# Four gathers at a time on GpSimd, each group held for two more query evictions of VectorE at a layer's head

## The chip, the core and the metric

The kernel runs on one core of a Trainium2 chip. The metric is device time in microseconds of one execution. A separate profiled execution, in which the hardware profiler records every instruction, gives the rows below.

## What is computed

A graph network on 3125 nodes and 100000 edges that are sorted by destination: four attention layers (8 heads of 16) and then one message layer. The part that the change touches is the attention over edges:

```python
def _transformer_conv(h, src, dst, Wq, bq, Wk, bk, Wv, bv, Ws, bs, Wbeta):
    q = (h @ Wq.T + bq)[dst].reshape(-1, HEADS, D_HEAD)
    k = (h @ Wk.T + bk)[src].reshape(-1, HEADS, D_HEAD)
    v = (h @ Wv.T + bv)[src].reshape(-1, HEADS, D_HEAD)
    alpha = jnp.sum(q * k, axis=-1) / float(np.sqrt(D_HEAD))
    amax = jax.ops.segment_max(alpha, dst, num_segments=n)
    ex = jnp.exp(alpha - amax[dst])
    denom = jax.ops.segment_sum(ex, dst, num_segments=n)
    a = ex / (denom[dst] + 1e-16)
    out = jax.ops.segment_sum((a[:, :, None] * v).reshape(-1, f), dst, num_segments=n)
    x_r = h @ Ws.T + bs
    beta = jax.nn.sigmoid(jnp.concatenate([out, x_r, out - x_r], axis=-1) @ Wbeta.T)
    return beta * x_r + (1.0 - beta) * out

for i in range(L):                      # L = 4
    res = h
    h = _transformer_conv(...)
    h = _layer_norm(h + res, ln_g[i], ln_b[i])
    h = gelu(h @ W1[i].T + b1[i]) @ W2[i].T + b2[i] + h
```

The message layer behind it gathers once more by source, adds what belongs to the destination, applies silu and takes the mean by destination.

## The kernel before

The nodes lie in NB = 25 blocks of 128. The edges are cut into 806 places of at most 128 edges, each place with edges of one block of destinations only. Sixteen places are a chunk (CHUNKS = 51; the last has six places), and a chunk has NG = 4 groups of G = 4 places.

All engines are programmed by hand, each with its own stream, and meet in semaphores. One attention layer runs so:

- **Head.** TensorE multiplies the 25 blocks with the key and value weights; VectorE evicts them (L1458) and SyncE stores them to `kv_table` in HBM in five pieces (L392, semaphore `tab_out`). Then come the queries: TensorE's `queries` (L966, two matmul passes a block, and a transpose, L970) alternates over two banks, and VectorE evicts each block in `begin_layer` (L1464) into `qs`, counting `q_ev`. TensorE's next block waits until `q_ev` says that the last-but-one is out of its bank. Behind the 25th eviction VectorE clears `acc` (L1467), makes the first one-hot tiles (L1249), takes 25 gate products (L1476), and multiplies chunk 0's keys with the queries (L1282) in four groups.
- **Gathers.** GpSimd (POOL) fetches each place's 128 rows of keys and values from `kv_table` with one indirect DMA (L508, in `gather_chunk`). The destination `slots` is a ring of RING = 4 chunks, so 64 gathers can run ahead. A gather waits for `tab_out` (the layer's table is stored), for `idx_in` (its indices are there), and per group for `slot_free`, which TensorE's last use of those four places releases (L825).
- **Chunks.** In `attend_step` of chunk n VectorE weighs chunk n's values (L1361), adds 16 partial sums to `acc` (L1265), and in between multiplies and sums chunk n+1's keys (L1282, L1288; each L1282 waits for `kv_in`, that is, four gathers landed, and for the spread queries of TensorE, L806). TensorE's add-ups are L825, ScalarE makes one-hot tiles.
- **Behind the last chunk** come gate, norm and feed-forward in five groups of five blocks, and the next layer's head.

Layer 0 is special: its gathers start as soon as the indices are in place, while VectorE still prepares the edge lists (L1607 to L1645); the first query eviction follows behind those. The message layer uses the same `gather_chunk` with `src_table`.

Of the kernel before, what the change touches and what calls it, by code (L numbers as in the profile page):

```python
# [25 lines left out]
L = 4  # L26
HEADS, DH = 8, 16
HID = HEADS * DH
NB = -(-N // P)
# [10 lines left out]
NG = CH // G  # L40
# [16 lines left out]
START = (RING - 1) * NG + 1  # L57
# [19 lines left out]
def build_program(nc, a, out):  # L77
    with ExitStack() as ctx:
# [3 lines left out]
        def sem(name):  # L82
            return ctx.enter_context(nc.semaphore(name))
# [166 lines left out]
        in_ps, in_act, s_ps, q_ev, h_ev = sem("in_ps"), sem("in_act"), sem("s_ps"), sem("q_ev"), sem("h_ev")  # L250
# [57 lines left out]
        def turn_of(l, i, k, j=0):  # L308

            return l * (FULL + (k < REM - 1 or (k == REM - 1 and j < LAST_NG))) + i  # L310
# [166 lines left out]
        @block.gpsimd  # L477
        def _(pool):


            for s in counted:
                pool.sem_inc(s, START)
            pool.wait_ge(su_idx, 1)
            for c in range(VC):
                pool.indirect_dma_start(row_sets[:, c, :], None, a["edge_t"],
                                        bass.IndirectOffsetOnAxis(ap=vti[:, c:c + 1], axis=0)).then_inc(su_rows, 16)
            uses = [[pool.alloc_register(f"uses{k}_{j}") for j in range(NG)] for k in range(RING)]
            for k in range(RING):
                for j in range(NG):
                    pool.reg_mov(uses[k][j], 0)  # L490

            def gather_chunk(k, turn, l, table, width, places=CH):
                groups = -(-places // G)
                used = [pool.snap(uses[k][j]) for j in range(groups)]
                if k == 2:
                    pool.wait_ge(su_termsd, 48)
                if k == 3:
                    pool.wait_ge(su_rstd, 16 * 2 * HEADS)
                pool.wait_ge(tab_out, 16 * NI * (l + 1))
                pool.wait_ge(idx_in[k], 16 * (turn + 1))  # L500
                for j in range(groups):
                    if isinstance(turn, int):
                        pool.wait_ge(slot_free[k][j], START + turn)
                    else:
                        pool.wait_ge(slot_free[k][j], START + used[j])
                        pool.reg_add(uses[k][j], uses[k][j], 1)
                    for t in range(j * G, min((j + 1) * G, places)):
                        pool.indirect_dma_start(slots[:, k, t, 0:width], None, table,  # L508
                                                bass.IndirectOffsetOnAxis(ap=idx[:, k, t:t + 1], axis=0))\
                            .then_inc(kv_in[k][j], 16)  # L510

            def gather_rest(l, table, width):
                for k in range(REM):
                    gather_chunk(k, turn_of(l, FULL, k), l, table, width, min(CH, PLACES - (RING * FULL + k) * CH))

            with pool.Fori(0, L) as l:
                with pool.Fori(0, FULL) as i:
                    for k in range(RING):
                        gather_chunk(k, turn_of(l, i, k), l, kv_table, KVW)
                gather_rest(l, kv_table, KVW)  # L520
            with pool.Fori(0, FULL) as i:
                for k in range(RING):
                    gather_chunk(k, turn_of(L, i, k), L, src_table, HID)
            gather_rest(L, src_table, HID)

            def root(sums, out, nth):

                pool.wait_ge(var_ans, START + 2 * nth)
                pool.tensor_tensor(guarded[:, :], sums, eps[:, :], ALU.add).then_inc(var_ans, 1)
                pool.wait_ge(var_ans, START + 2 * nth + 1)  # L530
                pool.tensor_tensor(out, guarded[:, :], half_power[:, :], ALU.pow).then_inc(var_ans, 1)

            pool.wait_ge(acc_done, START + CH * (L * CHUNKS + CHUNKS - 3))
            for i in range(NI):
                pool.memset(hidden[i][64:XW, :], 1.0).then_inc(hid_one, 1)
            for nth, (i, m) in enumerate(ASKED):
                pool.wait_ge(var_ready, START + nth + 1)
                root(var_of[2 * i + m], inv_of[2 * i + m], nth)
# [1271 lines left out]
```

## Time and profile before

| | us |
|---|---|
| time, median of 3 runs | 5614.84 (5613.83 to 5617.6) |
| profiled execution: span from the first to the last instruction | 7840.1 |
| PE / VectorE / ScalarE / POOL busy in it | 4625.7 / 4037.4 / 2769.9 / 3849.3 |
| mean granted TensorE clock in it | 0.679 |

For the profiled execution no time but its span is given. It is 40% longer than the runs without a profile. In the rows, "<-X" behind an idle time names what ended it; "remote" and "another core or an unknown queue" mean that the semaphore was raised by nothing that the profile can name, "issue" that the engine waited for nothing that it shows.

### The profile page before, as it was taken

The numbers are of one execution on the slowest core, as the hardware profiler recorded it, in microseconds if no ns is written. First come the engines' busy times: TensorE is split into PE (matmuls) and PEld (weight loads), VectorE is DVE, ScalarE is ACT, GpSimd is POOL, SyncE is SP. The second block draws the span as 40 slices with busy tenths as digits, with TensorE's granted clock in tenths as the row PEclk, the third lists the DMA queues.
The fourth block names the chain that finished last, engine by engine and source line by source line (L and its number), as shares of the span: only waits on it lengthen the run. The fifth ranks groups of instructions, "written<-read, shape, count | busy, mean of one in ns | idle before, by whom it ended". The sixth has DMA issues, their size and how long they took to land.

```text
span 7840.1 us, 106032 instructions
## 1 busy us (share of the span) xinstructions
PE 4625.7 (59%) x22831; PEld 3727.9 (48%) x22832; DVE 4037.4 (51%) x11107; ACT 2769.9 (35%) x6493; POOL 3849.3 (49%) x4066
## 2 busy tenths in 40 slices
PE   4555555655556556555555565555555656666667
PEld 2444444534444445344444453444444545555555
DVE  4555555645555556455555565555555553333334
ACT  1333333423333334233333342333333432323333
POOL 3555555335555553345555543455555425555553
PEclk6666666676666666766666667666666677877887
DMA  5222222222322222222223222222322211111111
GB/s 127 78 79 76 77 76 78 52 66 73 79 78 77 78 80 56 69 67 79 76 78 79 78 62 69 68 78 77 80 78 79 60 33 43 44 44 44 44 44 30
DMA packets 267188, 536.13 MB, mean 68 GB/s; under 512 B 116253, under 2 KB 148689, under 8 KB 266509
## 3 DMA queue, kind: packets, MB, share of 16 engines
q0 software_dynamic: 180992, 490.24, 23.6%
q1 hardware_dynamic: 78901, 35.89, 1.9%
q10 hardware_dynamic: 6936, 6.69, 0.3%
q14 instruction: 314, 2.57, 0.1%
q8 instruction: 45, 0.74, 0.0%
HBM read 512.41 MB, written 18.03 MB: 68 GB/s over the span
## 4 chain that ended last, share of the span: by engine, by line
PE 26%; another core or an unknown queue 26%; issue 20%; DVE 17%; ACT 5%; DVEq 4%; ACTq 1%; SPq 0%; DMA 0%; POOL 0%; POOLq 0%
PE bank L806 9%; PE bank L825 7%; DVE acc L1265 6%; ACT oh L556 2%; DVEq L333 2%; PE bank L797 2%; PE bank L851 2%; PE bank L810 1%; DVE alpha L1288 1%; PE bank L879 1%; DVEq L1265 1%; DVE slots L1361 1%; DVE oh L1249 1%; PE bank L1001 1%
## 5 line engine op out<-in xcount | busy, mean ns | idle before, releaser
L508 POOL DMA_INDIRECT slots<-kv_table,idx x3224 | 3065.2, 951 | 3133.0 <-PE bank L825 1275.8
L825 PE MATMUL bank<-slots,oh 128*128 128x136 f32 (+1 forms) x8060 | 1593.0, 351 | 569.1 <-DVE acc L1265 506.4
L806 PE MATMUL bank<-qs,ohT 128*128 x8080 | 1685.7, 356 | 235.1 <-ACT ohT L547 129.2
L825 PEld LDWEIGHTS bank<-slots,oh 128*128 128x128 f32 x8060 | 1411.7, 252 | 704.7 <-DVE acc L1265 608.2
L806 PEld LDWEIGHTS bank<-qs,ohT 128*128 128x128 f32 x8080 | 1434.4, 257 | 456.6 <-issue 434.4
L1265 DVE TENSOR_TENSOR acc<-acc,bank 128x136 f32 (+1 forms) x4030 | 1172.0, 291 | 614.6 <-PE bank L825 171.5
L1282 DVE TENSOR_TENSOR slots<-slots,bank 128x512 f32<-128x512 f32 x808 | 551.8, 683 | 1322.6 <-remote 1291.5
L547 ACT ACTIVATE ohT<-bank,miss 128x512 f32<-128x512 f32 x1010 | 676.7, 683 | 1367.9 <-PE bank L797 1234.5
L508 POOL DMA_INDIRECT slots<-src_table,idx x806 | 760.4, 943 | 756.9 <-DMA idx<-src_e 247.9
L843 PE MATMUL bank<-ident,alpha 128*128 128x128 f32 x204 | 93.7, 459 | 1487.2 <-DVE alpha L1288 1481.7
L556 ACT ACTIVATE oh<-iota,rel_e 128x128 f32<-128x128 f32 x3168 | 962.8, 387 | 0.0
L843 PEld LDWEIGHTS bank<-ident,alpha 128*128 128x128 f32 x204 | 36.4, 178 | 1527.5 <-DVE alpha L1288 1521.6
L569 ACT COPY f_in<-bank 1x256 f32<-1x256 f32 x204 | 73.6, 361 | 1464.0 <-PE bank L851 723.1
L1361 DVE TENSOR_TENSOR slots<-slots,bank 128x544 f32<-128x544 f32 x808 | 575.9, 713 | 5.0
L1288 DVE TENSOR_REDUCE alpha<-slots 128x32 f32<-128x512 f32 x808 | 549.1, 680 | 0.6
L797 PE MATMUL bank<-terms,spread 12*128 12x512 bf16 x1010 | 519.8, 524 | 40.2 <-issue 32.8
L1416 DVE TENSOR_TENSOR slots<-slots,bank 128x512 f32<-128x512 f32 x202 | 138.4, 685 | 769.6 <-remote 426.3
L628 ACT ACTIVATE slots<-slots 128x512 f32<-128x512 f32 x202 | 127.1, 630 | 962.5 <-DVE slots L1416 915.4
L560 ACT ACTIVATE oh<-oh 128x1024 f32<-128x1024 f32 x396 | 418.4, 1057 | 12.8
L810 PE MATMUL bank<-resets 128*128 128x128 f32 x1616 | 403.5, 339 | 11.5 <-issue 11.3
L810 PEld LDWEIGHTS bank<-resets 128*128 128x128 f32 x1616 | 333.5, 254 | 9.6 <-issue 9.3
L879 PE MATMUL bank<-ident,ex 128*128 128x128 f32 x204 | 96.8, 474 | 257.9 <-ACT ex L586 249.2
(257 smaller groups left out, 4079.5 us busy)
## 6 DMA issues: line engine op xcount, KB each, us to landing
slots<-kv_table,idx POOLq DMA_INDIRECT x3224
kv_table<-slots SPq DMA_DIRECT2D x20, 660.0 KB, 3.4
slots<-src_table,idx POOLq DMA_INDIRECT x806
resets<-flat_len ACTq DMA_DIRECT2D x51, 128.0 KB
idx<-src_e SPq DMA_DIRECT2D x255, 8.0 KB
terms<-flat_rel SPq DMA_DIRECT2D x255, 12.0 KB
resets<-flat_rst SPq DMA_DIRECT2D x2, 1551.0 KB
w<-in_w SPq DMA_DIRECT2D x8, 256.0 KB
```

The source lines that it names most:

```text
L508: pool.indirect_dma_start(slots[:, k, t, 0:width], None, table, bass.IndirectOffsetOnAxis(ap=idx[:, k, t:t + 1], axis=0))\
L547: act.activation(ohT[:, j % 2, :, :].rearrange("p a b -> p (a b)"), bank[j % 2][:, :], ACT.Relu, bias=miss[:, 0:1], scale=-1.0).then_inc(o ...
L556: act.activation(oh[:, k % 2, t, :], iota[:, :], ACT.Abs, bias=rel_e[:, bass.ds((prior + 1) * CH + t, 1)], scale=-1.0).then_inc(oh_far, 1 ...
L560: act.activation(tiles, tiles, ACT.Relu, bias=1.0, scale=-1.0).then_inc(oh_made, 1 + skipped)
L797: pe.matmul(bank[j % 2][:, :], spread[:, j, :], terms[:, k, :], start=True, stop=True)\
L806: mm = pe.matmul(o, ohT[:, j % 2, t, :], qs[:, blocks[j * G + t], 0:HID], start=True, stop=basis is None)
L810: mm = pe.matmul(o, rbf[:, k % 2, half, :], m_1c[:, q, :], start=False, stop=True)
L825: mm = pe.matmul(bank[6 + part % 2][:, o:o + width], oh[:, k % 2, t, :], slots[:, k, t, HID:HID + width], start=True, stop=True)
L1265: dve.tensor_tensor(a_t, a_t, bank[6 + part % 2][:, o:o + width], ALU.add)\
L1282: dve.tensor_tensor(keys, keys, bank[2 + j % 2][:, :].rearrange("p (t k) -> p t k", t=G), ALU.mult).then_inc(spread_used, counts_for(j, gr ...
L1288: dve.tensor_reduce(alpha[:, :, j * G:(j + 1) * G].rearrange("p h t -> p t h"), slots[:, k, j * G:(j + 1) * G, 0:HID].rearrange("p t (h d) ...
L1361: dve.tensor_tensor(vals, vals, bcl(exs[:, j * G:(j + 1) * G, :], VW), ALU.mult).then_inc(w_done, counts_for(j, groups))
```

## The change

One wait is added in `gather_chunk`, ahead of each group's wait for its slots, in the attention layers (`l is not L`; L is the message layer). Group j of ring slot k, counted 4k + j from 0 to 15, waits until 2(4k + j) of the layer's query evictions are done, at most 25.

```diff
                 for j in range(groups):
+                    if l is not L:
+                        pool.wait_ge(q_ev, START + NB * l + min(NB, 2 * (NG * k + j)))
                     if isinstance(turn, int):
                         pool.wait_ge(slot_free[k][j], START + turn)
                     else:
```

The streams of the other four engines are the same, row by row. On POOL, at the first two groups of the ring's first slot in the loop over chunks, before (`idx_in0`: indices of slot 0; `slot_free0_1`: group 1 of slot 0):

```order
L505 REGISTER_ALU [waits idx_in0]
L506 REGISTER_ALU [waits slot_free0_0]
L508 DMA slots<-kv_table,idx 128x264 x4
L505 REGISTER_ALU
L506 REGISTER_ALU [waits slot_free0_1]
L508 DMA slots<-kv_table,idx 128x264 x4
```

and with the change:

```order
L503 ISA [waits idx_in0]
L507 REGISTER_ALU [waits q_ev]
L508 REGISTER_ALU [waits slot_free0_0]
L510 DMA slots<-kv_table,idx 128x264 x4
L503 REGISTER_ALU
L507 REGISTER_ALU [waits q_ev]
L508 REGISTER_ALU [waits slot_free0_1]
L510 DMA slots<-kv_table,idx 128x264 x4
```

Each group has one register instruction with a wait on `q_ev` more; nothing has changed places. (Lines behind the edit are two higher in the changed kernel: gathers L510, evictions L1466, multiplies L1284.)

## Rows read from the trace of the kernel before

**Rows 1.** The page: span, GpSimd's busy time, the chain's shares by engine

```profile
span 7840.1 us, 106032 instructions
...
PE 4625.7 (59%) x22831; PEld 3727.9 (48%) x22832; DVE 4037.4 (51%) x11107; ACT 2769.9 (35%) x6493; POOL 3849.3 (49%) x4066
...
PE 26%; another core or an unknown queue 26%; issue 20%; DVE 17%; ACT 5%; DVEq 4%; ACTq 1%; SPq 0%; DMA 0%; POOL 0%; POOLq 0%
```

**Rows 2.** Costliest groups: busy us, mean ns of one, idle before, releaser

```profile
L508 POOL DMA_INDIRECT slots<-kv_table,idx x3224 | 3065.2, 951 | 3133.0 <-PE bank L825 1275.8
...
L1282 DVE TENSOR_TENSOR slots<-slots,bank 128x512 f32<-128x512 f32 x808 | 551.8, 683 | 1322.6 <-remote 1291.5
...
L508 POOL DMA_INDIRECT slots<-src_table,idx x806 | 760.4, 943 | 756.9 <-DMA idx<-src_e 247.9
```

**Rows 3.** Timeline, VectorE's key multiplies in layer 0's chunks: start, length

```profile
1013.62 0.69 DVE L1282 TENSOR_TENSOR slots<-slots,bank 128x512 f32<-128x512 f32 x1 [8.11 <-remote]
...
1506.62 0.69 DVE L1282 TENSOR_TENSOR slots<-slots,bank 128x512 f32<-128x512 f32 x1
...
1525.55 0.69 DVE L1282 TENSOR_TENSOR slots<-slots,bank 128x512 f32<-128x512 f32 x1
...
1546.87 0.69 DVE L1282 TENSOR_TENSOR slots<-slots,bank 128x512 f32<-128x512 f32 x1
```

**Rows 4.** Timeline of GpSimd where gathers of a layer end and begin

```profile
1493.41 0.94 POOL L508 DMA_INDIRECT slots<-kv_table,idx  x1 [0.30 <-issue]
1651.74 0.94 POOL L508 DMA_INDIRECT slots<-kv_table,idx  x1 [157.38 <-DMA kv_table<-slots]
...
6396.38 0.94 POOL L508 DMA_INDIRECT slots<-src_table,idx  x1 [168.71 <-DMA src_table<-slots]
...
7744.07 0.94 POOL L508 DMA_INDIRECT slots<-src_table,idx  x1 [0.30 <-issue]
```

**Rows 5.** Line L508: what it sat idle for, us and times

```profile
  DMA kv_table<-slots: 477.3, 3
```

**Rows 6.** Timeline, query evictions of layer 1

```profile
1650.04 0.42 DVE L1464 TENSOR_TENSOR qs<-bank,vec_qs 128x256 f32<-128x256 f32 x1 [3.62 <-PE bank L966]
...
1656.28 0.42 DVE L1464 TENSOR_TENSOR qs<-bank,vec_qs 128x256 f32<-128x256 f32 x1 [0.25 <-PE bank L966]
...
1700.37 0.42 DVE L1464 TENSOR_TENSOR qs<-bank,vec_qs 128x256 f32<-128x256 f32 x1 [8.67 <-remote]
1708.77 0.42 DVE L1464 TENSOR_TENSOR qs<-bank,vec_qs 128x256 f32<-128x256 f32 x1 [7.98 <-remote]
...
1741.72 0.76 DVE L1464 TENSOR_TENSOR qs<-bank,vec_qs 128x256 f32<-128x256 f32 x2 [2.39 <-PE bank L966]
```

**Rows 7.** Timeline of GpSimd, layer 1, first gather of group 9

```profile
1696.74 0.95 POOL L508 DMA_INDIRECT slots<-kv_table,idx  x1 [0.30 <-issue]
```

**Rows 8.** Windows: engines' busy us, PEclk, DMA share, GB/s

```profile
1690.00:1700.00 10.00, 1.44 (x3) 0.73 (x3) 0.42 (x1) 0.00 (x0) 7.56 (x9) 0.50 0.41 108
```

**Rows 9.** Timeline of GpSimd, head of layer 0

```profile
53.34 1.63 POOL L508 DMA_INDIRECT slots<-kv_table,idx  x1 [23.79 <-DMA idx<-src_e]
...
59.23 1.48 POOL L508 DMA_INDIRECT slots<-kv_table,idx  x1 [0.30 <-issue]
...
68.52 1.80 POOL L508 DMA_INDIRECT slots<-kv_table,idx  x1 [0.30 <-issue]
...
90.63 0.95 POOL L508 DMA_INDIRECT slots<-kv_table,idx  x1 [0.30 <-issue]
```

**Rows 10.** Timeline of VectorE, head of layer 0

```profile
67.41 1.09 DVE L1639 TENSOR_TENSOR oh<-oh 128x896 f32<-128x896 f32 x1 [5.26 <-DMA oh<-flat_dst]
...
73.39 0.74 DVE L1464 TENSOR_TENSOR qs<-bank,vec_qs 128x256 f32<-128x256 f32 x2
...
151.31 0.97 DVE L1464 TENSOR_TENSOR qs<-bank,vec_qs 128x256 f32<-128x256 f32 x2 [0.24 <-PE bank L966]
...
164.53 0.69 DVE L1282 TENSOR_TENSOR slots<-slots,bank 128x512 f32<-128x512 f32 x1
```

## The prediction

> **What bounds the kernel now.** I read the page first. The profiled span is 7840.1 us [rows 1], the median of the runs 5614.8 us: 2225 us, 40%, lie between an execution with the profiler and one without. Before any row is used, it has to be settled which of them are the kernel's own. The chain that ended last puts 26% of the span, 2038 us, on "another core or an unknown queue" [rows 1], though the program runs on one core. 7840 - 2038 = 5802, near the median. The reader should see those unnamed waits in two places. In the chunks VectorE's key multiply waited 1291.5 us in all for "remote" [rows 2], about 8 us a chunk [rows 3]. In the heads the query evictions, undisturbed up to the ninth (1650.04 to 1656.28, 0.78 us each), come 8.4 us apart later on (1700.37, 1708.77), again for "remote" [rows 6], while POOL gathers without a pause and the DMA engines are busy only 0.41 of the time [rows 8]. So what POOL's stream disturbs is the arrival of semaphores, not bandwidth. If all these waits ran at full size without the profiler, the runs would take 7840 us; so they must be mostly an effect of the profiled execution.
>
> What bounds the runs, then? Take the waits away and two rates remain. POOL: a gather takes 0.95 us [rows 2] and 0.30 us pass to the next [rows 9], 1.25 us, hence 16 x 1.25 = 20.0 us a chunk. VectorE, TensorE and ScalarE together: where gathers have ended, one chunk's first multiply follows the last chunk's after 1525.55 - 1506.62 = 18.9 us [rows 3]. POOL is the slower by 1.1 us a chunk, though the profile, with 27 us a chunk, shows it half idle. As a test I add up POOL's stream alone: first gather at 53.3 [rows 9]; 3224 + 806 = 4030 gathers x 1.25 = 5037.5 [rows 2]; pauses between layers 477.3 [rows 5] and 168.7 [rows 4]. Of each pause some 50 us are lead that a bound POOL would not have: layer 0's last gather starts at 1493.41 [rows 4], its multiply at 1546.87 [rows 3], and some 3 us would remain for a gather to land (an estimate); so -200 for four. Behind the last gather come 7840.1 - 7744.1 = 96 us [rows 1, 4], 50 of them lead again, 46 left. Sum: 53 + 5038 + 477 + 169 - 200 + 46 = 5583 us, 0.6% under the median. A kernel bound by the other engines at 19.8 us a chunk would give the median as well, so the test is consistent, not proof.
>
> **The change, part by part.**
>
> *Added instructions.* One register instruction with a wait, per group. In the trace such instructions pass while earlier gathers are still being worked off: the 0.30 us ahead of a group's first gather are the same as inside a group [rows 7, 9]. What hides them is the sequencer's lead over the gathers; without it each would cost well under the 0.30 us. Cost 0, at most 806 groups x 0.1 = 80 us if nothing hid them, which the equal gaps speak against.
>
> *Turns after the first, and the message layer.* Once a layer's 25 evictions are done the waits hold at once; the message layer has none. 0.
>
> *Layers 1 to 3.* Group m may start when 2m evictions are done. POOL needs 4 x 1.25 = 5.0 us a group; two undisturbed evictions need 1.6 us, and they begin (1650.04) before the first gather (1651.74) [rows 4, 6]. The wait never binds. 0. In the profiled execution it binds late: group 9 started at 1696.74 [rows 7], its 18th eviction began at 1700.37, and when group 10 with its twenty was due, 5 us on, the 19th had not begun [rows 6]. That changes the profile, not the runs.
>
> *Layer 0.* This is where the change costs. Gathers begin at 53.34 and run on; group 1 starts at 59.23 [rows 9]. VectorE is still at the edge lists, its first two evictions start at 73.39 and end at 74.13 [rows 10]. Group 0 asks for no eviction, group 1 must wait for those two. From a passed wait to a gather's start I allow 0.8 us: the ends are 0.30, the gap between two gathers, and 1.25, a gather's whole period, and 0.8 is their middle. Group 1 moves from 59.2 to 74.9, +15.7 us, and all behind it on POOL moves along, since later groups (5.0 us each) never wait for evictions (1.6 us for two). Two of the moved gathers took 1.48 and 1.80 us beside VectorE's work on the edge lists instead of 0.95 [rows 9]; behind 74 us there is no such work: -1.4 us. VectorE waited 5.26 us for the reload of `flat_dst` [rows 10], which shared the DMA engines with groups 1 and 2; without them it may come sooner, between 0 and 2 us, and I take 1 (group 1 is a part of the traffic, not most of it). Sum: 15.7 - 1.4 - 1 = 13.3 us later on POOL.
>
> The Trainium skill, page SBUF — State Buffer, section "SBUF: two separate sides", says that a VectorE instruction on two ports locks GpSimd out from writing descriptors; the slow gathers beside VectorE's conversions agree, and by that rule alone the 1.4 us come back.
>
> *Does the delay reach the end?* Chunk 0's first multiply is at 164.53 in the profile; 25 evictions at 0.78 take 19 instead of 79 us (73.39 to 152.28) [rows 6, 10], so without disturbance it comes at about 105. The fourth multiply of chunk 1, some 23 us behind it, is at 128; its group's gathers start at 90.63 [rows 9], last 5 us and land at about 99. Lead 29 us before, 15 to 16 with the change. POOL loses 1.07 us a chunk against the others, 52 us over 49 chunks: the lead is used up in both kernels, POOL then sets the pace, and the whole 13.3 us arrive at the end. The ring is not full in between: slot 0 comes free about one chunk's time behind the first multiply, at some 125, while POOL's 64 gathers last till 135. Predicted: 5614.8 + 13.3 = 5628 us, +0.24%. Against the profiled execution the same term would be hidden, since there POOL waits for slots.
>
> **The rivals.**
>
> *A, hidden.* The lead of layer 0 takes the delay. It decides at 19.4 us: with a chunk of the other engines above 20 - 29/49 = 19.4 us the loss shrinks, above 20 - 15/49 = 19.7 it is zero. For it: the median is met as well by 19.8 us a chunk, and layer 0's 50 chunks of the profile (164.53 to 1546.87, 27.6 us each) [rows 3, 10], less 1291.5/202 = 6.4 us of waits [rows 2], are 21.2 and not 18.9. Against it: those 21.2 still hold the smaller unnamed waits and a TensorE that idles in between, 21.2 throughout would give more than the median, and POOL's sum meets the median from below. Time 5612 to 5618.
>
> *B, faster.* The slow evictions are real in the runs too, and the groups' waits loosen POOL's stream. Place: heads of layers 0, 1, 2. It decides at 2.5 us an eviction: only if they are slower does a group of 5.0 us wait for two. Price: in layer 1 the last seven evictions, 34 us (1708.77 to 1742.5) [rows 6], would go at 2.5 each, 17 us saved; the same in layer 2; in layer 0, where it binds from about the eighth, some 30; in layer 3 nothing. Together 60 us: 5555. Were all stalls gone, 60 + 73 + 73 + 30, it would be 5380, but the first eight groups of a layer stay as they are. For it: the rows of the heads, as they stand. Against it: the median. A stall a tenth as large as the profile's fits the median as well, and gives nothing, since evictions then stay under 2.5 us.
>
> The Trainium skill, page NOTIFIC — the notification-queue block, section "Constraints, capacities, measured rates", holds that recording an implicit record costs the engine zero cycles; by that rule the stalls would be the kernel's own, and B would be the case at 5555 us. The 2225 us between the profiled span and the median are against it here.
>
> *C, the change does nothing at all.* The order of POOL's instructions shows the waits; only a first eviction far sooner than 73 us without the profiler would make them free. Same as A in time.
>
> **How the numbers follow.** A measurement of this kernel can tell 0.2%, 11.2 us, from no change. POOL bound with the delay in full, 5624 to 5632: 0.47, of which 0.40 above 11.2 us. Partly or wholly hidden (A, C): 0.40, same. B: 0.13, faster. Some unforeseen loss, such as a pause in layers 1 to 3: 0.02 more on the slow side, taken from A. So faster 0.13, same 0.45, slower 0.42. The likeliest single case is the first. The range 5605 to 5638 holds it and A with what their terms leave open; it leaves out most of B and a larger loss.
>
> **What the changed profile would show.** Group 1 of layer 0 starting at about 75 us and not 59; layers 1 and 2 with pauses on POOL from group 9 on, and their last evictions closer together; the multiplies of the chunks still waiting 8 us for "remote". Its span may well fall by tens of us while the runs get slower. If the median stays within 5 us, the step that fails is POOL as the bound; if it falls by more than 11 us, it is the reading of the stalls as the profiler's.

## The result and the profile after

| | before | with the change |
|---|---|---|
| median of the runs, us | 5617.6 (9 runs) | 5632.39 (9 runs, 5630.05 to 5633.69) |
| profiled execution: span, us | 7840.1 | 5631.5 |
| profiled execution: own time, us | not given | 5633.27 |
| mean granted TensorE clock in it | 0.679 | 0.766 |

The ratio is 1.0025, with a 95% interval of 1.0016 to 1.0034: slower by 14 us, 0.25% (14.8 us by the two medians). Forecast was 5628.0, +13.3 us, with a range from 5605 to 5638. One of the nine executions of the kernel before took 9772.95 us; the ratio leaves it out.

The first thing to see is that the profiled execution of the changed kernel takes what its runs take: the span is 5631.5 us and not 40% more. The page of the changed kernel: span, busy times, the chain's shares, and the groups that answer to [rows 1] and [rows 2]:

```profile
span 5631.5 us, 106744 instructions
...
PE 4316.8 (77%) x22831; PEld 3520.3 (63%) x22832; DVE 4029.5 (72%) x11107; ACT 2773.2 (49%) x6493; POOL 3847.0 (68%) x4066
...
POOL 63%; issue 24%; PE 5%; DVE 4%; POOLq 2%; ACT 1%; DMA 1%; DVEq 0%; SPq 0%; ACTq 0%
...
L510 POOL DMA_INDIRECT slots<-kv_table,idx x3224 | 3061.7, 950 | 1360.9 <-issue 977.1
...
L510 POOL DMA_INDIRECT slots<-src_table,idx x806 | 761.6, 945 | 369.4 <-issue 245.3
...
L1284 DVE TENSOR_TENSOR slots<-slots,bank 128x512 f32<-128x512 f32 x808 | 551.7, 683 | 96.4 <-DMA slots<-kv_table,idx 90.7
```

No unnamed wait is left in the chain. GpSimd's gathers are 63% of it, and most of the 24% "issue" are the 0.30 us between them. VectorE's key multiplies idled 96.4 us where [rows 2] had 1322.6, and what they wait for is named here: the gathers. GpSimd is the engine that sets the pace. That the unnamed waits are gone is not the work of the change, as the kernel before, profiled once more, shows below.

Timeline of GpSimd in the changed kernel, head of layer 0 (start, length, in brackets the idle time before it), beside [rows 9]:

```profile
53.33 1.52 POOL L510 DMA_INDIRECT slots<-kv_table,idx  x1 [23.56 <-DMA idx<-src_e]
...
57.66 1.16 POOL L510 DMA_INDIRECT slots<-kv_table,idx  x1 [0.30 <-issue]
74.14 0.94 POOL L510 DMA_INDIRECT slots<-kv_table,idx  x1 [15.31 <-DVE qs L1466]
75.38 0.95 POOL L510 DMA_INDIRECT slots<-kv_table,idx  x1 [0.30 <-issue]
...
79.14 0.95 POOL L510 DMA_INDIRECT slots<-kv_table,idx  x1 [0.30 <-issue]
80.39 0.94 POOL L510 DMA_INDIRECT slots<-kv_table,idx  x1 [0.30 <-DVE qs L1466]
```

The fifth gather, the first of group 1, idles 15.31 us and is released by a query eviction. Group 2 starts at 79.14, 0.30 us behind the gather before it: its wait costs nothing. At 80.39, in the middle of group 2 and ahead of no added wait, the profile names an eviction once more, but the gap is the usual 0.30 us. Once group 1 has started, GpSimd idles more than 1 us ahead of a gather only between the layers. The evictions that released group 1 are the pair at 72.55 in VectorE's timeline of the same kernel:

```profile
66.62 1.09 DVE L1641 TENSOR_TENSOR oh<-oh 128x896 f32<-128x896 f32 x1 [4.58 <-DMA oh<-flat_dst]
...
72.55 0.75 DVE L1466 TENSOR_TENSOR qs<-bank,vec_qs 128x256 f32<-128x256 f32 x2
```

And the query evictions of layer 1 in the changed kernel, all 25 of them (min, median and max ns, first and last start), which answer to [rows 6]:

```profile
L1466 DVE TENSOR_TENSOR qs<-bank,vec_qs x25: 423/425/426, 1191.8 to 1208.0; 128x256 f32<-128x256 f32 x25
```

From the first start to the last they take 16.2 us, 0.68 us each, with none of the 8 us waits of [rows 6].

### The profile page after: what moved, and what is told of

It is laid out like the page before. It is cut to its first block, busy times and chain, and to the rows that moved or that the text cites. A ratio compares the mean times of both kernels' runs of the same rounds, so it can differ in the third digit from the quotient of the medians.

```text
span 5631.5 us, 106744 instructions
## 1 busy us (share of the span) xinstructions
PE 4316.8 (77%) x22831; PEld 3520.3 (63%) x22832; DVE 4029.5 (72%) x11107; ACT 2773.2 (49%) x6493; POOL 3847.0 (68%) x4066
## 4 chain that ended last, share of the span: by engine, by line
POOL 63%; issue 24%; PE 5%; DVE 4%; POOLq 2%; ACT 1%; DMA 1%; DVEq 0%; SPq 0%; ACTq 0%
POOL slots L510 63%; PE bank L1003 1%; PE bank L968 1%; PE bank L992 1%; PE bank L960 1%; POOLq L508 1%; DVE acc L1267 0%; POOLq L507 0%; POOLq L503 0%; DVE slots L1514 0%; POOLq L494 0%; DVE slots L1520 0%; DVE slots L1460 0%; POOLq L500 0%; DVE slots L1518 0%
## 5 line engine op out<-in xcount | busy, mean ns | idle before, releaser
L510 POOL DMA_INDIRECT slots<-kv_table,idx x3224 | 3061.7, 950 | 1360.9 <-issue 977.1
L827 PE MATMUL bank<-slots,oh 128*128 128x136 f32 (+1 forms) x8060 | 1508.0, 336 | 320.6 <-DVE acc L1267 318.4
L808 PE MATMUL bank<-qs,ohT 128*128 x8080 | 1638.5, 349 | 109.0 <-DVE slots L1284 36.5
L827 PEld LDWEIGHTS bank<-slots,oh 128*128 128x128 f32 x8060 | 1326.2, 238 | 441.1 <-DVE acc L1267 401.7
L808 PEld LDWEIGHTS bank<-qs,ohT 128*128 128x128 f32 x8080 | 1389.6, 250 | 306.8 <-issue 284.8
L510 POOL DMA_INDIRECT slots<-src_table,idx x806 | 761.6, 945 | 369.4 <-issue 245.3
L1284 DVE TENSOR_TENSOR slots<-slots,bank 128x512 f32<-128x512 f32 x808 | 551.7, 683 | 96.4 <-DMA slots<-kv_table,idx 90.7
L799 PE MATMUL bank<-terms,spread 12*128 12x512 bf16 x1010 | 483.9, 488 | 75.9 <-issue 66.8
L812 PE MATMUL bank<-resets 128*128 128x128 f32 x1616 | 365.3, 314 | 0.0
L812 PEld LDWEIGHTS bank<-resets 128*128 128x128 f32 x1616 | 299.4, 231 | 0.0
L1340 DVE TENSOR_TENSOR_SCAN fwd<-resets,icol,bank 128x128 f32<-128x128 f32 (+1 forms) x204 | 97.8, 480 | 242.6 <-issue 237.1
L853 PE MATMUL bank<-ident,fwd 128*1 128x128 f32 x204 | 63.4, 311 | 242.2 <-DVE bwd L1302 203.8
L799 PEld LDWEIGHTS bank<-terms,spread 12*128 12x128 bf16 x1010 | 121.0, 123 | 198.7 <-issue 167.4
```

What stands on the lines that cost most here:

```text
L799: pe.matmul(bank[j % 2][:, :], spread[:, j, :], terms[:, k, :], start=True, stop=True)\
L808: mm = pe.matmul(o, ohT[:, j % 2, t, :], qs[:, blocks[j * G + t], 0:HID], start=True, stop=basis is None)
L812: mm = pe.matmul(o, rbf[:, k % 2, half, :], m_1c[:, q, :], start=False, stop=True)
L827: mm = pe.matmul(bank[6 + part % 2][:, o:o + width], oh[:, k % 2, t, :], slots[:, k, t, HID:HID + width], start=True, stop=True)
L1284: dve.tensor_tensor(keys, keys, bank[2 + j % 2][:, :].rearrange("p (t k) -> p t k", t=G), ALU.mult).then_inc(spread_used, counts_for(j, gr ...
```

## The experiments

Each kernel ran beside runs of the kernel before on the same chip. The medians of these were 5619.82 us (25 runs) for the waits that hold, layer 0 alone, layers 1 to 3 alone and the kernel before once more; 5622.6 (15 runs) for all 25 evictions, the two with a slower VectorE and the first of the earlier gathers; and 5618.22 (15 runs) for the last.

### The kernel before, profiled once more

No edit.

> The kernel before, unchanged, for a second profiled execution. Theory (POOL bound; the unnamed waits belong to the one execution that was profiled): span near 5615 us, group 1 of layer 0 at about 59 us, 25 evictions a head in some 17 us, the chunks' multiplies waiting for gathers. Rival (the waits come with the profiler, always): span near 7840 us again.

Measured: 5619.07 us, span 5617.2. The page of this execution:

```profile
span 5617.2 us, 106032 instructions
...
PE 4307.6 (77%) x22831; PEld 3513.2 (63%) x22832; DVE 4031.6 (72%) x11107; ACT 2773.2 (49%) x6493; POOL 3847.5 (68%) x4066
...
POOL 63%; issue 24%; PE 5%; DVE 4%; POOLq 2%; DMA 1%; ACT 1%; DVEq 0%; SPq 0%; ACTq 0%
...
L508 POOL DMA_INDIRECT slots<-kv_table,idx x3224 | 3062.3, 950 | 1343.2 <-issue 980.9
```

and its timeline of GpSimd:

```profile
52.50 1.62 POOL L508 DMA_INDIRECT slots<-kv_table,idx  x1 [22.97 <-DMA idx<-src_e]
...
58.38 1.49 POOL L508 DMA_INDIRECT slots<-kv_table,idx  x1 [0.30 <-issue]
...
67.68 1.69 POOL L508 DMA_INDIRECT slots<-kv_table,idx  x1 [0.30 <-issue]
...
135.11 0.95 POOL L508 DMA_INDIRECT slots<-kv_table,idx  x1 [0.30 <-issue]
...
1063.95 0.95 POOL L508 DMA_INDIRECT slots<-kv_table,idx  x1 [0.30 <-issue]
```

This is the profile of before that should be laid beside the one after. VectorE, ScalarE and GpSimd are busy within 6 us of [rows 1]. TensorE's 4625.7 us at a mean granted clock of 0.679 became 4307.6 us at 0.766, and none of the unnamed waits is there. Gathers pause for more than 1 us only four times, between the layers. So the 2225 us over the median were not what a profiler does to this kernel: they belonged to that one execution. Everything below is compared with this profile. Span to span the change costs 14.3 us.

### Waits that always hold

```diff
-                        pool.wait_ge(q_ev, START + NB * l + min(NB, 2 * (NG * k + j)))
+                        pool.wait_ge(q_ev, START + NB * l + 0)
```

> The change with every threshold put back to the previous layer's evictions, so that the instructions are there and never wait. Theory (the added instructions are hidden): within 2 us of the kernel before, ratio 1.000. Rival (each added instruction costs POOL some 0.02 us or more): 806 x 0.02 = 16 us, as much as the whole loss.

Measured: 5621.49 us (11 runs), ratio 1.0002 (0.9993 to 1.0011), span 5620.4. The added instructions cost nothing that the runs can tell: it is the waiting in the threshold that costs.

### Layer 0 alone, and layers 1 to 3 alone

Layer 0 is taken out of GpSimd's loop over layers in both:

```diff
-                    if l is not L:
+                    if isinstance(l, int) and l == 0:
...
-                    if isinstance(turn, int):
+                    if isinstance(turn, int) and l is L:
...
-            with pool.Fori(0, L) as l:
+            def gather_layer(l):
...
+            gather_layer(0)
+            with pool.Fori(1, L) as l:
+                gather_layer(l)
```

and for layers 1 to 3 alone the condition is `not isinstance(l, int)`. The second pair of lines keeps layer 0's waits for slots what they were, now that its `l` and `turn` are plain numbers.

> The waits in layer 0 alone (layer 0 stands ahead of the loop over layers). Theory (all of the loss is layer 0's): +14 us, ratio 1.0025. Rival (layers 1 to 3 share in it): clearly less than 14.

> The waits in layers 1 to 3 alone, with layer 0 ahead of the loop as in the run with layer 0 only. Theory: 0, within 2 us, ratio 1.000. Rival: what the other run lacks to 14 us, or that the layer ahead of the loop costs by itself.

Measured: layer 0 alone 5633.23 us (9 runs), ratio 1.0023 (1.0013 to 1.0033), span 5633.3, group 1 at 75.0. Layers 1 to 3 alone 5620.35 us (11 runs), ratio 1.0003 (0.9994 to 1.0012), span 5617.2. The whole loss is layer 0's, as far as the runs can tell, and neither the waits of the other layers nor taking layer 0 out of the loop costs anything that can be told.

### All 25 evictions in layer 0

The same loop, and in layer 0 every group but the first waits for the whole head of queries:

```diff
+                    if isinstance(l, int) and l == 0 and NG * k + j > 0:
+                        pool.wait_ge(q_ev, START + NB)
```

> A larger dose in layer 0 alone: every group but the first waits for all 25 query evictions, which end at about 89 us. Group 1 starts at about 89 in place of 58.4, +30.5 us. Theory (POOL bound, delay arrives one for one): +29 us after the 1.4 us of slow gathers come back, ratio 1.005. Rival (some lead takes the first part of a delay, or the loss is not the delay): less than twice the change's 14 us.

Measured: 5654.55 us (5 runs, 5644.09 to 5657.95), ratio 1.0057 (1.0044 to 1.0071), span 5642.3: +32 us by the medians, +25 by the spans. GpSimd's timeline there:

```profile
57.68 1.18 POOL L510 DMA_INDIRECT slots<-kv_table,idx  x1 [0.30 <-issue]
89.70 0.95 POOL L510 DMA_INDIRECT slots<-kv_table,idx  x1 [30.85 <-DVE qs L1470]
...
1093.66 0.95 POOL L510 DMA_INDIRECT slots<-kv_table,idx  x1 [0.30 <-issue]
```

Group 1 starts 31.3 us later than before (89.70 - 58.38), the last gather of layer 0 starts 29.7 us later (1093.66 - 1063.95); 0.8 us of both is that this execution's first gather was late (53.26 against 52.50). Twice the hold, about twice the loss (the one profiled execution, the shortest of the five, gives 25, the median 32): a hold in GpSimd's stream arrives at the end nearly whole.

### The same change where VectorE is the slower

To both kernels, ahead of the scans of each attention chunk, a VectorE reduction that nobody uses:

```diff
+                dve.wait_ge(filled, START + g)
+                dve.tensor_reduce(filler[:, :], bc(iota[:, :], 24), axis=X, op=ALU.add).then_inc(filled, 1)
```

> The kernel before with a useless reduction of 3072 elements a chunk on VectorE (about 3 us, of which some fall into its wait), in the attention layers only. It lifts the other engines' pace from 18.9 to about 21 us a chunk, above POOL's 20.0. Both theories: +100 to +250 us. It is the reference for the next run.

> The changed kernel with the same useless reduction. Theory (the delay costs only because POOL sets the pace): the same time as the kernel before with the reduction, within 3 us. Rival (the delay costs whatever the bound): 14 us above it.

Measured: 6192.78 us without the change (ratio 1.1015, 1.1000 to 1.1030, span 6191.0) and 6194.96 with it (1.1019, 1.1004 to 1.1034, span 6191.4). The chain's shares on the page of the one without the change:

```profile
issue 26%; PE 25%; DVE 24%; POOL 12%; DVEq 6%; ACT 5%; DMA 0%; ACTq 0%; POOLq 0%; SPq 0%
```

The reduction, in its list of instructions (min, median and max ns, first and last start):

```profile
L1340 DVE TENSOR_REDUCE filler<-iota x204: 3352/3353/3354, 114.1 to 5027.3; 128x24 f32<-128x3072 f32 x102
```

And what GpSimd's gathers sat idle for in the first 1300 us (us, times):

```profile
  issue: 225.6, 728
  PE bank L827: 121.9, 76
```

They idled 121.9 us for slots that TensorE's add-ups release. GpSimd now waits for the others, and its share of the chain falls from 63% to 12%. In the pair the change holds group 1 just as long (74.08 against 58.36), yet costs 2.2 us by the medians, inside their intervals, and 0.4 us by the spans. So the delay is a loss only because GpSimd sets the pace.

The run without the change missed its own forecast, +100 to +250 us: it took 570 us more. The forecast put the others' pace at 21 us a chunk; from the first multiply of layer 0 (100.92) to the first of its last chunk (1223.06) it is 22.4. That the filler cost 570 us for 204 x 3.35 = 684 us of VectorE fits the same picture: 20.0 us a chunk less the others' 19.4 (below) give 0.6 x 204 = 122 us that were free.

### The first gather earlier

Two edits of the kernel before that start its gathers sooner. In the first, VectorE copies the turned indices of the first 128 places (chunks 0 to 7) ahead of the relative positions, and SyncE loads the first four chunks' indices once those are there:

```diff
+            take(0)
             for c in range(VC):
                 ins = dve.tensor_scalar(r_rel[:, c, :], rows_f[:, c, :], vt[:, 1, c:c + 1], None, ALU.subtract)
             ins.then_inc(su_turn, 1)
-            for k in range(VC):
+            for k in range(1, VC):
                 take(k)
...
-            sp.wait_ge(su_taken, VC)
+            sp.wait_ge(su_taken, 1)
```

> The opposite of the change, on the kernel before: VectorE takes the first 128 turned index columns ahead of its work on the blocks of destinations, and SyncE loads the first four chunks' indices once those are there. Layer 0's gathers should start about 3 to 4 us earlier. Theory: 3 to 4 us faster than before, ratio 0.9994. Rival (gathers that start earlier only wait elsewhere): no difference.

Measured: 5623.44 us (11 runs), ratio 0.9999 (0.9990 to 1.0008), span 5619.8. No gain, although the first gather starts 3.2 us sooner. Its GpSimd:

```profile
49.29 0.95 POOL L508 DMA_INDIRECT slots<-kv_table,idx  x1 [19.75 <-DMA idx<-src_e]
...
135.98 0.95 POOL L508 DMA_INDIRECT slots<-kv_table,idx  x1 [4.66 <-DMA idx<-src_e]
```

The 65th gather, the first of the ring's second turn, waits 4.66 us for chunk 4's indices: the head start is given back. SyncE issues that load only behind its wait at L441 for the "far resets", a transfer that VectorE's scans need later. How long that takes, the chain of the run with waits that always hold tells:

```profile
88.98 40.37 DMA resets<-flat_rst
```

In the second, on top of the first, SyncE issues chunk 4's indices ahead of that wait. For this the rest of layer 0's loads stands ahead of SyncE's loop over layers, in the order they had; of the edit only the start is shown:

```diff
-            sp.wait_ge(su_far, 32)
+            sp.wait_ge(spread_used, START + NG)
+            load_sources(0, RING)
+            sp.wait_ge(su_far, 32)
+            load_terms(0, RING)
```

> Edit: the kernel before, with group 0's index block computed alone and released first (as in n1_indices_earlier), and SyncE loading chunk 4's indices ahead of its wait for the far resets. Theory (GpSimd's stream sets the end): group 0's first gather starts at about 49.3 us as in n1, the row of group 16 no longer waits for indices (it was at 135.98 after a wait of 4.66 us in n1) and starts at about 132; the last gather of layer 0 ends some 3 us earlier than before (1064.9) and the run is 3 to 4 us faster, a ratio of 0.9994, at the edge of what the rounds can tell. Rival (the multiplies' slots or another wait takes the place of the indices): group 16 starts at 135 to 136 again with another name behind the wait, and the time is that of the kernel before within 1 us.

Measured: 5613.39 us (11 runs, 5609.26 to 5618.68) against 5618.22, ratio 0.9992 (0.9983 to 1.0001), span 5613.7. GpSimd's timeline:

```profile
49.48 1.05 POOL L522 DMA_INDIRECT slots<-kv_table,idx  x1 [19.96 <-DMA idx<-src_e]
...
131.53 0.95 POOL L522 DMA_INDIRECT slots<-kv_table,idx  x1 [0.30 <-issue]
...
1060.19 0.95 POOL L522 DMA_INDIRECT slots<-kv_table,idx  x1 [0.30 <-issue]
```

and the list of VectorE's key multiplies in layer 0:

```profile
L1296 DVE TENSOR_TENSOR slots<-slots,bank x202: 674/680/690, 100.6 to 1070.7; 128x512 f32<-128x512 f32 x101
```

The pause for indices is gone, and the last gather of layer 0 starts 3.8 us sooner than before (1060.19 against 1063.95). But layer 1's first gather starts at 1178.33, where the kernel before has it at 1178.40. In layer 0 no key multiply waits for a gather any more, and its 202 multiplies span 970.1 us, against 970.8 in the kernel before: the other engines set layer 0 now. Its last multiply still starts 2.4 us sooner (1070.73 against 1073.17), since its first did (100.58 against 102.42), but the stretch from there to layer 1's first gather took 107.6 us against 105.2, and why is open. So neither theory as written is all of it. The gathers came early as the first said; in layer 0 the gain then ran into another bound, as the second said, though not into the one that it named. The 3.5 us between the spans appear behind layer 0, where this edit changes nothing, and the interval still holds 1. If this is a gain at all, it is one that the runs don't settle, and so no version here is shown to beat the kernel before.

## Why the prediction was right, and where it was not

**The reading of the profile of before.** "They must be mostly an effect of the profiled execution": right for the runs, which is what the forecast needed, but wrong if it is read as what profiling does. Both later profiled executions, 5617.2 and 5631.5 us, are within 2 us of their own times. What failed is the division of the 2225 us between the profiler and the kernel, which also gave rival B its case. There was a third possibility, which the prediction did not name: neither the kernel nor the profiler, but that one execution. The Trainium skill, page NOTIFIC — the notification-queue block, section "Constraints, capacities, measured rates", has recording at zero cycles for the engine. These two executions agree with it (span 5617.2 beside 5619.07). Why the one execution was disturbed is open. The 9772.95 us in the list of runs show that another execution can be far longer too, but there is no profile of it, and whether its cause is the same is not known. Whether the change would help or hurt in such an execution was not tried.

**GpSimd as the bound.** Right: 63% of the chain. The sum of its stream holds term by term in the clean profile. First gather 52.5, predicted 53. Gathers 3823.9 busy and 1226.2 between them, 5050, predicted 5038. Pauses between layers 339.4 + 125.6 = 465, predicted 477 + 169 - 200 = 446. Behind the last gather 5617.2 - 5567.6 = 49.6, predicted 46. They make 5617, where the prediction had 5583: the missing 34 us are gathers that are a little longer (12), pauses from which 45 us of lead go and not 50 (19), and the tail (3). The prediction left 3 us between the last gather of a layer and its last multiply; in layer 0 of the clean profile it is 9.2 (1063.95 to 1073.17). GpSimd's idle list for the gathers in the kernel before, clean, is where the pauses stand:

```profile
  issue: 1226.2, 4025
  DMA kv_table<-slots: 339.4, 3
  DMA src_table<-slots: 125.6, 1
```

**Added instructions: 0.** Right (ratio 1.0002 with waits that always hold).

**Layers 1 to 3: 0.** Right (1.0003). With the change the profile names the query evictions behind the three pauses ahead of layers 1 to 3, but these are 113.6, 114.5 and 113.4 us long, against 113.5, 114.6 and 111.3 before, and with the waits in layers 1 to 3 alone 112.9, 111.9 and 113.8. But "layers 1 and 2 with pauses on POOL from group 9 on" did not come, since the slow evictions it rested on were that execution's; head 16 us, not 92.

**Layer 0: 13.3 us.** Right in each term. The two executions have to be laid on their first gathers, since everything in the one with the change began 0.8 us later (53.33 against 52.50). So counted, group 1 moves from 5.88 to 20.81 us, by 14.9 us; predicted were 15.7, less 1 for the reload, 14.7. (The plain difference, 74.14 - 58.38 = 15.8, holds the late start.) Wait to gather: the evictions end at 73.30, the gather starts at 74.14, 0.84 us where 0.8 was allowed. Slow gathers given back: 1.4 predicted; in the clean profile they are 1.49 and 1.69 against 0.95, so 1.3. By the Trainium skill, page SBUF — State Buffer, section "SBUF: two separate sides", a VectorE instruction on two ports keeps GpSimd from writing descriptors; with the gathers moved behind the conversions these lengths are gone (0.94 and 0.95 for the 30 from 74.14 to 110.39), which agrees. Reload of `flat_dst` sooner: 1 predicted; its wait fell from 5.09 to 4.58 us, and the first eviction, counted from the first gather, from 19.94 to 19.22, so 0.7, which is in the 14.9 already. Sum: 14.9 - 1.3 = 13.6 us. The last gather of layer 0 starts 14.6 us later, 13.8 without the late start. That late start is also in the 14.3 us between the spans. Why it came is open: SyncE's store of the layer's table already starts at 30.58 against 29.95, as it does in two executions that hold nothing (30.59 and 30.33, the two with the first gather earlier).

**Does it reach the end?** The answer was right, three of its numbers were not. First, the pace of the other engines. Predicted were 18.9 us a chunk, hence 1.07 us lost a chunk. The run whose layer 0 waits for no gather gives it free of GpSimd: from the first multiply at 100.58 to the first of the last chunk at 1067.97, 967.4 us over 50 chunks, 19.35. The loss is 0.65 a chunk, 32 us in layer 0, against a lead of 28 (126.68, the last multiply of chunk 1, less the prediction's 99). So in the kernel before the multiplies catch up with GpSimd only near the end of layer 0, as VectorE's key multiplies of layer 0 show there, with what they sat idle for, and the first of the nine that wait:

```profile
L1282 DVE TENSOR_TENSOR slots<-slots,bank x202: 675/684/690, 102.4 to 1073.2; 128x512 f32<-128x512 f32 x101
...
  DMA slots<-kv_table,idx: 10.2, 9
...
878.24 0.69 DVE L1282 TENSOR_TENSOR slots<-slots,bank 128x512 f32<-128x512 f32 x1 [0.42 <-DMA slots<-kv_table,idx]
```

Rival A named 19.4 us a chunk as the point from which the delay begins to shrink. The chunk is at 19.35. That the 13.3 us arrived whole was in part luck: the forecast stood just on the right side of an edge that it took to be half a microsecond away, with 4 us of loss over lead where it had counted 23. With a slightly slower VectorE, part of the 14 us would have gone into layer 0's lead, and the run with the filler shows where that ends, at 0.4 us.

Second, "lead 15 to 16 with the change". The same list for the changed kernel:

```profile
L1284 DVE TENSOR_TENSOR slots<-slots,bank x202: 675/680/689, 101.4 to 1087.0; 128x512 f32<-128x512 f32 x101
...
  DMA slots<-kv_table,idx: 19.0, 12
```

and one of these multiplies from its timeline:

```profile
127.41 0.69 DVE L1284 TENSOR_TENSOR slots<-slots,bank 128x512 f32<-128x512 f32 x1 [7.53 <-DMA slots<-kv_table,idx]
```

Chunk 1's second multiply waits 7.53 us for gathers whose last ended on GpSimd at 98.84 (97.89 + 0.95). They landed some 28 us later and not the 3 us later that the prediction allowed. SyncE is released from its wait for the far resets at just that time (it issues the next load at 127.76). So it looks as if gathers that the change pushes past 86 us run beside that transfer of 40 us and land late because of it. It cost nothing in the sum only because VectorE's pace did not matter.

Third, "the ring is not full in between", with slot 0 free at some 125 and 64 gathers lasting till 135. The slot is free, but the next thing a gather needs, chunk 4's indices, isn't: SyncE issues them at 126.09 in the clean profile of before, and in two other runs with this head GpSimd did wait 2.77 us (waits that always hold) and 2.59 us (layers 1 to 3 alone) for them. With the change the 65th gather comes at 149.36, well behind them. So of the delay 0 to 2.8 us are covered by a wait that is there anyway; that is within what the runs scatter.

**The rivals.** A fell on the measured loss of 14 us, narrowly, as said. B fell: the evictions take 0.68 us each, and two for a group of 5 us never hold. C fell: 15.31 us of idle time ahead of group 1. Of what the changed profile was to show, group 1 "at about 75" came (74.14); multiplies still waiting 8 us for "remote" and a falling span compared with a clean one did not.

## What to carry to other kernels

Before any wait of a profile is used, lay its span beside the unprofiled times; if they differ by more than the runs scatter, take a second profile, and until then trust only what adds up to the unprofiled time, such as the busy time of one engine plus the gaps that it has even where nothing disturbs it. A hold put into the stream of the engine that sets the pace reaches the end nearly one for one, here 15.3 us of hold for 14 us of time, and comes to nothing for the same hold where another engine was slower; starting that stream sooner is not the mirror image, as the gain stops at the next bound, here after less than 1 us in layer 0. For a lead, count when data land and not when they are issued: here one group landed 28 us behind its last gather where 3 had been allowed.

## What the runs showed of the hardware

- A whole execution can be 40% longer (7840.1 against 5617.2 us) with the busy times of VectorE, ScalarE and GpSimd the same within 6 us, a mean granted TensorE clock of 0.679 against 0.766, and waits that no named event ends.
- Gathers of 128 rows take 0.95 us on average plus 0.30 to the next on GpSimd, the same with the DMA engines busy 0.24 of the time (4600 to 5500 us, kernel before) and 0.71 (99 to 125 us). But beside the transfer of 40 us the multiply that needed four of them waited until some 28 us after the last had ended on GpSimd (127.41 against 98.84); in the run with all 25 evictions chunk 0's multiplies waited 9.47 and 12.30 us for them:

```profile
112.13 0.69 DVE L1288 TENSOR_TENSOR slots<-slots,bank 128x512 f32<-128x512 f32 x1 [9.47 <-DMA slots<-kv_table,idx]
125.84 0.69 DVE L1288 TENSOR_TENSOR slots<-slots,bank 128x512 f32<-128x512 f32 x1 [12.30 <-DMA slots<-kv_table,idx]
```

- That the transfer of the far resets is what delays them is argued and not shown. It rests on the two times agreeing (127.41 and 127.76). In the run with all 25 evictions the later of the two waits ends near that transfer's end too (125.84, SyncE's next load at 127.96), but the earlier ends at 112.13, well inside it, 17.7 us behind the last of its four gathers on GpSimd. Moving that load was not tried.
